# Running the expert layer on tokens sorted by expert instead of on all tokens

## What is computed

```python
x = x + tanh(g_xattn) * cross_attention(layernorm(x), ctx_1024)       # 16 heads, logits clipped
xf = layernorm(x)
logits = xf @ wr + br                                                  # 4 experts
topk_vals, topk_idx = top_k(logits, 2)
gates = softmax(topk_vals)
h = gelu(einsum('nd,edh->enh', xf, w1) + b1)                           # every expert, every token
y = einsum('enh,ehd->end', h, w2) + b2
c = einsum('eh,ehd->ed', gelu(b1), w2) + b2
out = einsum('nk,nkd->nd', gates, y[topk_idx] - c[topk_idx] + c.sum(axis=0))
x = x + tanh(g_ffn) * out
```

## Time and profile before

| | |
|---|---|
| median of 3 runs | 1250.18 us (1249.36 to 1250.47) |
| the profiled execution | 1251.45 us |
| its span in the trace | 1249.7 us |
| mean granted TensorE clock | 0.994 |
| PE / DVE / ACT / POOL busy | 96% / 81% / 46% / 32% |
| HBM read, written | 26.11 MB, 2.10 MB |

### The profile page before, as it was taken

The page is one execution under the profiler, slowest core; times in us unless marked ns, Lnnn a source line. Parts: engine busy times, 40 slices in busy tenths (PEclk is TensorE's granted clock), DMA queues, the critical chain, the costliest instruction groups (busy, mean ns, idle before and its releaser), DMA issues.

```text
span 1249.7 us, 22921 instructions
## 1 busy us (share of the span) xinstructions
PE 1200.6 (96%) x8289; PEld 813.3 (65%) x8289; DVE 1007.3 (81%) x1688; ACT 578.9 (46%) x1044; POOL 399.9 (32%) x409
## 2 busy tenths in 40 slices
PE   5799999999999999999999999989999999999997
PEld 3555555564555655555555555555899999999896
DVE  7699999988999898899989899997685664665554
ACT  4554567555556655455755554554322222222221
POOL 5333664433376333346534334552100000000000
PEclk9999999999999999999999999999999999999999
DMA  7000000000000000010000000022011020000001
GB/s 194 1 9 27 18 27 10 18 10 11 18 24 29 10 9 10 11 34 23 13 10 17 15 10 9 9 77 85 1 34 35 1 67 0 1 1 0 18 17 34
DMA packets 33070, 29.65 MB, mean 24 GB/s; under 512 B 9144, under 2 KB 31808, under 8 KB 32960
## 3 DMA queue, kind: packets, MB, share of 16 engines
q1 hardware_dynamic: 32944, 28.21, 7.3%
q10 hardware_dynamic: 16, 0.00, 0.0%
HBM read 26.11 MB, written 2.10 MB: 23 GB/s over the span
## 4 chain that ended last, share of the span: by engine, by line
PE 80%; DVE 11%; issue 3%; POOL 3%; ACT 1%; SPq 0%; DMA 0%; POOLq 0%; DVEq 0%; ACTq 0%
PE pv L1230 14%; PE sc L1216 12%; PE kv L1161 5%; PE kv L1163 5%; PE kv L1162 5%; PE sc L1161 5%; PE sc L1162 5%; PE sc L1163 5%; PE mi L1161 4%; PE mi L1163 3%; PE mi L1162 3%; DVE acc L827 3%; PE tr L1202 3%; PE mi L1240 2%; PE pv L1161 1%
## 5 line engine op out<-in xcount | busy, mean ns | idle before, releaser
L632 ACT ACTIVATE prob<-sc 128x1024 f32<-128x1024 f32 x256 | 249.1, 1029 | 221.8 <-PE sc L1216 219.1
L1230 PE MATMUL pv<-prob,val 128*32 128x512 f32 x2048 | 247.1, 600 | 2.7 <-DVE prob L812 2.7
L493 POOL TENSOR_TENSOR rot_s<-k_raw,sinb 128x256 f32<-128x256 f32 x128 | 107.3, 838 | 388.6 <-ACT k_raw L580 388.6
L1216 PE MATMUL sc<-q_hid,big 64*128 64x512 f32 x1536 | 212.7, 409 | 4.7 <-issue 4.7
L1216 PEld LDWEIGHTS sc<-q_hid,big 64*128 64x128 f32 x1536 | 134.3, 184 | 113.2 <-issue 60.0
L812 DVE TENSOR_SCALAR prob<-prob 128x1024 f32<-128x1024 f32 x256 | 183.3, 728 | 27.7 <-ACT prob L632 23.9
L827 DVE TENSOR_TENSOR acc<-acc,prob 128x1024 f32<-128x1024 f32 x128 | 204.9, 1621 | 0.0
L1082 DVE TENSOR_SCALAR q_hid<-prob,gb 128x512 fp32r<-128x512 f32 x128 | 62.6, 489 | 104.8 <-ACT prob L713 103.6
L497 POOL TENSOR_TENSOR rot_c<-rot_c,rot_s 128x256 f32<-128x256 f32 x128 | 124.7, 974 | 35.2 <-DVE rot_c L801 19.0
L1230 PEld LDWEIGHTS pv<-prob,val 128*32 128x32 f32 x2048 | 56.8, 109 | 112.3 <-issue 82.7
L713 ACT ACTIVATE prob<-sc,b1t 128x512 f32<-128x512 f32 x64 | 44.1, 689 | 171.0 <-PE sc L1163 171.0
(11 more groups left out here) (170 smaller groups left out, 2432.7 us busy)
## 6 DMA issues: line engine op xcount, KB each, us to landing
val<-in_L_ffn_w SPq DMA_DIRECT2D x6, 1024.0 KB, 5.1
rows<-in_ctx SPq DMA_DIRECT2D x32, 128.0 KB, 2.1
w_raw<-in_L_xattn_Wq SPq DMA_DIRECT2D x16, 256.0 KB, 2.7
w_raw<-in_L_xattn_Wo SPq DMA_DIRECT2D x64, 64.0 KB, 1.9
prob<-in_L_xattn_Wkv SPq DMA_DIRECT2D x8, 256.0 KB, 4.8
xacc<-in_x SPq DMA_DIRECT2D x4, 512.0 KB, 4.6
val<-in_L_ffn_w SPq DMA_DIRECT2D x4, 512.0 KB, 3.8
out<-xacc SPq DMA_DIRECT2D x4, 512.0 KB, 2.9
```

The source lines that it names most:

```text
L493: g.tensor_tensor(rot_s[:].rearrange("p (h a c) -> p h a c", h=4, a=2), kh[:, :, ::-1, :], sinb[:, t].unsqueeze(1).to_broadcast([P, 4, 2, ...
L632: a.activation(prob[:, s % 2, i, :], sc[i][:], ACT.Exp, scale=DH ** -0.5).then_inc(exp_done[i], 1)
L1216: last = mm(sc[i][:, h * N:(h + 1) * N], kst[rows_h, u % 2, j, lk, t * P:(t + 1) * P], q_sp[rows_h, p % 2, lq, :], start=lk + lq == 0, sto ...
L1230: last = mm(pv[g * 32:(g + 1) * 32, :], val[:, u % 2, 2 * c + i, at:at + 32], prob[:, s % 2, i, h * N:(h + 1) * N], start=c == 0 and i == ...
```

## The change

Tokens of batches 0 to 2 (1536 tokens, 3072 token-expert pairs) are sorted by expert into 15 tiles of 256 rows: 12 would hold the pairs, 3 more make room for the partly filled last tile of an expert. The number is fixed; all 15 are always computed. Their normalised rows are written to their places in a DRAM buffer by 24 indirect transfers issued from POOL (128 rows of 1 KB each), read back as tiles, run through the expert that owns the tile, and the results written to a second DRAM buffer and fetched by 24 indirect gathers from POOL. Batch 3 goes through all 4 experts as before. So there are 19 jobs of 8 steps: 15 of 256 rows, 4 of 512.

- The biases and statistics of a batch move from the last batch's steps to steps s >= 4 of u = 3 (bias) and of the next batch's u = 0 (statistics); `rows_norm`, `x_turn`, `router` of batches 0 to 2 move to i = 9 to 16.
- New in the last batch's attention: ranking at i = 17, a count of slots on PE (13 small matmuls) at i = 18, places, gates and the tiles' owners on DVE at i = 18 to 21, scatters on POOL at i = 20 to 25, four rows normalised again at i = 24, a 3.9 MB clearing of the buffer at i = 8.
- Weights are loaded for each job (2 MB, expert number read by SP from SBUF), rounded by ACT (`w_round`, 8 chunks of 512 columns a job), low part by POOL (`w_low`, 8 chunks a job); DVE's `split` and POOL's `x_low` are gone.
- Gelu is applied in place in PSUM; DVE reads PSUM.
- The loops on the chip are gone; all jobs are written out.

The core of the diff:

```diff
+            def w_round(job, chunk):
+                half, c = chunk // 4, chunk % 4
+                cols = slice(c * 512, (c + 1) * 512)
+                if c == 0:
+                    act.wait_ge(f_ldw[job % 2][half], 16 * ((job + 1) // 2))
+                    if job > 1:
+                        act.wait_ge((h_mm, y_mm)[half], (job - 1) * MT)
+                a.activation(w_of(job, half, 0)[:, cols], raw_of(job, half)[:, cols], ACT.Copy).then_inc(w_high[half], 1)
...
+            def w_low(job, chunk):
...
+                pool.wait_ge(w_high[half], (job - 1) * 4 + c + 1)
+                low = g.tensor_tensor(w_of(job, half, 1)[:, cols], raw_of(job, half)[:, cols],
+                                      w_of(job, half, 0)[:, cols].bitcast(F32), ALU.subtract)
+                if c == 3:
+                    low.then_inc(w_ready[half], 1)
...
+            for job in range(1, JOBS):
+                for chunk in range(2 * 4):
+                    w_low(job, chunk)
+                    if job == 3 and chunk == 0:
+                        rows_scale(EARLY, B * NT)
+                if SLOT_TILES < job < JOBS - 1:
+                    for n in range(EARLY):
+                        gather((job - SLOT_TILES - 1) * EARLY + n)
...
+                if last and R_RANK + 3 <= i < R_RANK + 7:
+                    for n in range(3):
+                        scatter((i - R_RANK - 3) * 3 + n)
+                if last and i == R_RANK + 7:
+                    for n in range(12, 16):
+                        scatter(n)
+                if last and i == R_RANK + 8:
+                    for n in range(16, 2 * EARLY):
+                        scatter(n)
...
+            for k in range(SLOT_TILES):
+                if k:
+                    store_slots(k - 1)
+                    load_weights(k + 2)
+                if k + 2 < SLOT_TILES:
+                    load_slots(k + 2)
...
-                a.activation(hid[:, m % 4, :], hb[m % 4], ACT.Gelu, bias=b1t[:, e * MT + m:e * MT + m + 1]).then_inc(h_act, 1)
+                a.activation(h, h, ACT.Gelu, bias=bias).then_inc(h_act, 1)
...
+                src, dst = hb[n % 4][:, 0:w], hid_sp[:, n % 4]
+                v.tensor_scalar(dst[:, 0, 0:w], src, c, None, ALU.subtract).then_inc(h_high, 1)
                 dve.wait_ge(h_high, n + 1)
+                v.scalar_tensor_tensor(dst[:, 1, 0:w], src, c, dst[:, 0, 0:w].bitcast(F32),
                                        ALU.subtract, ALU.subtract).then_inc(h_ready, 1)
...
+                    last = three(hb[n % 4][:, 0:TS] if routed else hb[n % 4],
+                                 lambda l: w1v[job % 2][:, l, k, m * P:(m + 1) * P],
+                                 lambda l: x_k[:, job % 2, l, k, :] if routed else x_t[:, l, k, :], k == 0, k == KT - 1)
...
+                for i in range(2 if e < 0 else NT):
+                    bank = yb[1][job % 2] if e < 0 else yb[e % 2][i // 2]
...
+            for n in range(JOBS * MT):
+                job, m = n // MT, n % MT
+                outputs(n)
+                if n + 3 < JOBS * MT:
+                    hidden(n + 3)
+                if job + 1 < SLOT_TILES and m == 0:
+                    if job > LATE_TILE:
+                        pe.wait_ge(f_xready, min(job - LATE_TILE, 2))
+                    pe.wait_ge(s_ready, job + 1)
+                    slots_turn(job + 1)
```

More of the change, by code:

```diff
@@ L724, in _ @@
-                if n == MT + 4:
-                    act.wait_ge(f_diff, 1)
-                    a.activation(f_tmp, f_logit, ACT.Exp).then_inc(f_exp, 1)
-            for e in range(1, E):
-                with act.Fori(0, B) as t:
-                    for m in range(MT):
-                        gelu(t * MT + (e * B * MT + m), e, m)
+                if job + 1 < SLOT_TILES and m == 3:
+                    slots_round(job + 1)
+                if job in (LATE_TILE, LATE_TILE + 1) and m == 6:
+                    x_out(EH + job - LATE_TILE)
@@ L733, in _ @@
+                if job == LATE_TILE + 3 and m == 0:
+                    act.wait_ge(f_diff, 2)
+                    a.activation(f_tmp[:, EARLY:, :], f_logit[:, EARLY:, :], ACT.Exp).then_inc(f_exp, 1)
         @block.vector
@@ L1145, in _, with copy_slots @@
-            for e in range(1, E):
-                biases(e)
-                for t in range(B):
-                    for m in range(MT):
-                        hidden((t + e * B) * MT + m, e, m)
-                        if t == 1 and e + 1 < E:
-                            split(e + 1, m)
-                    combine(e, t, t % 2)
+            def copy_slots(k):
+                dve.wait_ge(y_mm, (k + 1) * MT)
+                wait(dve, y_stored[k % 2], 16 * (k // 2))
+                v.tensor_copy(y_st[:, k % 2, :], yb[1][k % 2]).then_inc(y_copied, 1)
@@ new lines, in _ @@
+            denominators(B - 1, PAIRS - 1)
+            pe.wait_ge(p_ready, PIECES)
+            for n in range(3):
+                hidden(n)
+            for n in range(JOBS * MT):
+                job, m = n // MT, n % MT
+                outputs(n)
[4 more added lines that the diff above has]
+                        pe.wait_ge(f_xready, min(job - LATE_TILE, 2))
+                    pe.wait_ge(s_ready, job + 1)
+                    slots_turn(job + 1)
+                if n == 5:
@@ L1442 @@
+                    router(EH + job - LATE_TILE, mi, 0)
+                if job >= SLOT_TILES and m == 3:
+                    biases(job - SLOT_TILES)
 INPUTS = ["x", "ctx_1024", "g_xattn", "g_ffn", "L0_xattn_cos", "L0_xattn_sin", "L0_xattn_ln_lat_g", "L0_xattn_ln_lat_b",
```

771 lines of the change are left out of this document (504 added, 267 removed).

## The result

The changed kernel takes 1204.3 us (median of 4 runs, 1203.28 to 1211.33), the kernel before 1249.77 us in the runs beside it (median of 4). The ratio is 0.9649 with a 95% interval of 0.9612 to 0.9686: 45 us less, where 63 were forecast. The profiled execution took 1203.28 us, with a span of 1201.5 and a mean clock of 0.987.

The account below looks back on a forecast made before the run. PE was taken as the bound, the expert layer being pure matmul rate. 1251.45 - 69 (expert layer) + 6 (attention) = 1188.5 us profiled, 1187 as median; range 1166 to 1228.

Parts of the forecast that it names:

- The forecast's own ends: Whole kernel: 1166 (job at 11.95, no late gathers, attention at -4) to 1205 (job at 13.3, attention +12).
- PE's rate and the routed job: Sorted tiles: 256-column matmuls 0.12 us apart; PE's work 11.95 us a job, 12.6 with waits.
- POOL's chunk at 1.3: Sorted jobs: one 512-column weight low part a step takes POOL 1.3 us, under the limit of 1.49.
- 0.65 a job for the transfer loop and small chains: Sorted jobs: 0.65 us on top of PE's 11.95, for the closed load loop and DVE's small chains.
- Indirect transfers at 1.4: POOL, batch 3: 1.4 us per gather; each set of 12 makes weights about 3.6 late, 8 us in all.
- The tail at 8.8: End of the expert layer: stays at 8.8 us, from 386.4 less 360, 11.4 and 8, with rounding and final sums.
- Attention, +6: Attention: net +6 us, from -10 in the last unit, +9 on DVE, +3 in other batches, +4 for scatters.
- 6 half batches at 1.1 us on PE: Last batch's attention: work moved into i = 9 to 16, at about 1.1 us of PE per half batch.
- 10 less 4: Last attention unit: -10 us as rows_norm, transposes and router leave; +4 as scatters delay weight pieces and ACT.
- transfers never set a job: Rival, sorted jobs: the load loop sets the job at 15 us, +36, 1223 in all; chance 0.18.
- indirect transfers at 2.1: Rival, POOL: 2.1 us each, late gathers +16 and the scatters' tail +8, 1211 in all; chance 0.14.
- POOL did not bind: Rival, sorted jobs: low-part chunks at 2.28 make jobs 18.2 us, 1276 in all, slower; chance 0.09.

Follow-up runs that it names:

- e6: Against e5: DVE's late ranking cut into four parts over four steps, the sum of b2 into three steps; 1182.39 us, ratio 0.9468.
- e1: Against the changed kernel: all 12 collects moved into the last job, where POOL has no work; 1198.38 us, ratio 0.9584.
- e2: Against the changed kernel: POOL makes low parts of only 64 of each weight chunk's 512 columns; 1180.64 us, ratio 0.9447.
- e5: e1 and e3 together, plus POOL's 24 gathers issued one by one behind low parts from the middle of job 15; 1190.43 us, ratio 0.9525.
- e8: Against the changed kernel: the 11 slot-count matmuls issued twice in step i = 18; 1202.43 us in a single run.
- e3: Against the changed kernel: POOL's last 8 scatters placed behind the low parts of the first two weight pieces; 1191.63 us, ratio 0.9531.
- e9: Against e6: two and three scatters placed between the low parts of the last weight pieces on POOL; 1182.95 us, ratio 0.9453.

## Why the prediction was right, and where it was wrong

The time, 1204.3, is inside the range, and the direction was right for the reason given: the matmul columns of the expert layer. The size of the gain was not: 45 us where 63 were forecast. The range reached to 1228 for two rivals that did not happen. The forecast's own ends, added up again from the terms given, are 1159 (1187 - 10 - 8 - 10) and 1203 (1187 + 10 + 6), not 1166 and 1205; the measured time is just above them. By its steps:

- **PE's rate and the routed job**: right. Matmuls of 256 columns 0.12 apart, and jobs of 11.95 wherever nothing disturbed them (jobs 3, 10, 12, 13).
- **POOL's chunk at 1.3**: right (1.30), with POOL 84% busy and under PE. The reason given, that DVE reads PSUM there, holds as well, but only one half of the question was asked: what DVE does to POOL. What POOL does to DVE was costed at nothing, although show DVE's two additions at 2.90 beside POOL, and two alone take 2.35 (e6, 864.78 to 867.13). e1 prices it at 8.9 us in jobs 16 and 17 (3.4 of them came back in the last job), and e6 at 7.6 in the routed jobs; e2's 24 us is the price of the low parts' whole length, the wait behind the gathers and what the forecast allowed for small chains included. It is the largest term that the working lacks.
- **0.65 a job for the transfer loop and small chains**: the right sum (200.6 against 199) from errors that cancel. The loop cost nothing, since several jobs ran at PE's own 11.95. The attention's leftover, forecast at 10, was 5.2 in jobs 0 to 2; batch 3's own transposes and routers, which the sum has not, come to 3.1 in jobs 4 and 5. The small chains cost more than assumed: `rank_gates` was priced by the earlier trace rows at 0.22 an operation, a row from before, where POOL was idle, and `b2_sum` was not priced; beside `w_low` one operation of 16 columns took 1.12. e6 takes 8 us back by cutting them up.
- **ACT and DVE in the routed job**: Gelu 0.45 (0.47 forecast), high part 0.48 (0.42), low part 0.48 (0.48), a rounding chunk 0.62 (0.65).
- **Indirect transfers at 1.4**: right, 1.3 to 1.55 with the issue. That POOL would be late with the weights in jobs 16 and 17 was right too: 6.0 us between e1 and e5 (8 were forecast). What was missing beside them is the hold of the collects, 8.9 us less in those two jobs when they left (e1).
- **The tail at 8.8**: measured 8.5 (33.9 with the last job's 25.4). The subtraction given for it comes to 7.0, so that this term is right by luck.
- **Attention, +6**: the step that failed most, +14.2. Its terms: the other batches cost nothing in this profile (exponentials at 707.26 and 707.64 at i = 8) where 3 was forecast; the profiles of other runs with the same code have that exponential between 706.29 and 710.76, so that 0 and 3 cannot be told apart. For i = 8 to 24 the sum had +9, drawn from DVE's load; it measured 16.3. The prediction named 6 half batches at 1.1 us on PE and then did not add them, though PE was busy 49.2 of the 49.3 us of unit 1 (and 47.4 of 50 in the earlier trace rows): their 64 records are unit 1's growth (PE's busy time rose by 7.9 us, the unit by 8.4). In unit 2 step i = 18 was 11.9 us long, some 5 more than its neighbours: PE had 3.0 us of count matmuls in it and was idle for 1.9 before them. e8 shows that these matmuls stand on the path, at a price above their duration. The last unit was to give 10 less 4 and gave 1.7: POOL's scatters, forecast as a delay of 4 us, cost ACT 8.6, and when they no longer did (e3) the low parts held DVE in their place.
- **Rivals**: transfers never set a job, with 60% of the DMA time busy (one wait of 0.28 for a tile, at 1034.11, is all that PE shows); indirect transfers at 2.1 did not happen, the longest took 1.82 (1.97 in e9); POOL did not bind. The rule of the Trainium skill ("SBUF — State Buffer", Who interferes with whom) that POOL's descriptor writes are shut out by DVE's 2-port modes would show as scatters longer than gathers: they are, 0.97 to 1.82 in attention against 0.99 to 1.15 in the gathers' block, so up to 0.85 each. What else could make a scatter longer than a gather was not separated.

Put right, the attention would have read 0 + 8.4 + 8 - 2 = +14, and jobs 16 and 17 +15 in place of 8. What the change left on the table, e6 shows: 1182.4 us, better than both kernels, with the same mathematics and the orders of three queues changed.

## What to carry to other kernels

When work moves to POOL, price it on DVE too: here a back-to-back run of POOL operations on SBUF shut out a DVE operation on SBUF for the whole run or nearly so, so put something else (here a gather) between them, keep small DVE chains short in any one step, or let DVE read PSUM. Where an engine is full in a window, count what is moved there in full, whatever the other engines' slack: 7.9 us more on PE made unit 1 8.4 longer. And a block of transfers on POOL's queue delays all that stands behind it; issued one by one between due work, the same transfers were free.

## What was not expected of the hardware

- **Runs, not single instructions.** DVE was held for 7.6 us by a run of POOL operations of 1.3 us each (the collect of 8.09), and 4.8 by two of 2.4 (e3: 7.17 in place of 2.35). It met operations with two operands in SBUF and the clamp with one (e6: 5.77). In the four long holds that met a run at its start (8.09, 7.98, 7.17, 5.77) the DVE operation's recorded start lies before the run's, by 0.22 to 0.51 us. DVE operations that read one operand from PSUM kept their 0.48 beside the same runs (L1374).
- **A clock that follows short waits.** After 3.80 us of waiting PE ran matmuls at 0.21 for 3 us (job 6), and small matmuls (22 records of 4 to 44 columns) were followed by a stretch at the 1.2 GHz level without a wait (e8: 4.84 for the work of 2.66). A wait on PE cost more here than its length.
- **Chance alignments of 9 us.** Job 17 took 34.78 or 25.8 with the same code, as its collects fell beside one or the other kind of POOL work. A comparison of two such kernels says something of an edit only after the jobs are compared one by one.
